# Two cross attentions whose first batch is pulled ahead of batches 1 and 2, with the first loads cut in pieces on two queues

## The reference

```python
x = x + cross_attention_0(layernorm(x), ctx, tau, delta)   # 16 heads of 16 channels, 120 keys
x = x + encoder_block(layernorm(x))                        # self attention, then one of 8 experts per token
x = x + cross_attention_1(layernorm(x), ctx, tau, delta)   # as the first, other weights
x = x + permuted_experts(layernorm(x))                     # groups of 32 tokens, 128 sets
# inside a cross attention:
q = heads(z @ Wq.T + bq); k = heads(c @ Wk.T + bk); v = heads(c @ Wv.T + bv)
scores = (q @ k.T * tau + delta) / 4
out = (softmax(scores) @ v) @ Wo.T + bo
```

## Time and profile before

| | |
|---|---|
| median of 3 runs | 977.71 us (977.0 to 981.29) |
| profiled execution | 980.43 us, span 978.6 us |
| granted TensorE clock, mean | 0.875 |
| busy: PE, DVE, ACT, POOL | 800.0, 501.8, 344.4, 242.9 us |
| first cross attention, first scores at | 60.41 us |
| second cross attention, first scores at | 705.56 us |

### The profile page before, as it was taken

How to read it: one execution, slowest core, us unless ns; L and a number is a source line. 1 busy time by engine, 2 the same in 40 slices (tenths; PEclk the granted TensorE clock), 3 DMA queues, 4 the chain that set the end, 5 groups by cost and what they waited for, 6 DMA issues and landing times.

```text
span 978.6 us, 16232 instructions
## 1 busy us (share of the span) xinstructions
PE 800.0 (82%) x6103; PEld 605.3 (62%) x6103; DVE 501.8 (51%) x1223; ACT 344.4 (35%) x627; POOL 242.9 (25%) x242
## 2 busy tenths in 40 slices
PE   3557989899999999831799999935479888997998
PEld 2335766566665665531699999924356666675865
DVE  3544577876778765422112212125556886444743
ACT  1323544544544544400222222203044456443211
POOL 1512333322234321211211111026234532112000
PEclk9768989999999999965799999978587799657999
DMA  4959465754463663328454566346835550332001
GB/s 150 122 70 190 81 90 72 96 78 79 67 141 63 74 132 126 130 86 129 148 200 163 185 189 171 103 106 77 105 70 78 88 83 25 121 155 88 1 33 54
DMA packets 66896, 103.29 MB, mean 106 GB/s; under 512 B 21614, under 2 KB 56942, under 8 KB 61662
## 3 DMA queue, kind: packets, MB, share of 16 engines
q1 hardware_dynamic: 64403, 97.07, 47.2%
q0 software_dynamic: 2416, 5.19, 2.9%
HBM read 56.61 MB, written 7.28 MB: 65 GB/s over the span
## 4 chain that ended last, share of the span: by engine, by line
PE 64%; DVE 11%; DMA 8%; ACT 5%; issue 4%; POOL 4%; SPq 3%; DVEq 0%; POOLq 0%; ACTq 0%
PE PS L724 9%; PE U L735 8%; PE U L641 7%; PE MB L574 6%; PE MB L662 5%; PE MB L652 4%; PE PS L627 4%; PE MB L604 4%; PE MB L804 3%; PE MB L590 3%; PE MB L814 2%; SPq L1460 2%; DMA y<-yb,pos 2%; DVE nma L1070 2%; DMA QKa<-mTa 2%
## 5 line engine op out<-in xcount | busy, mean ns | idle before, releaser
L1070 DVE TENSOR_REDUCE nma<-MB 128x2 f32<-128x512 f32 (+1 forms) x192 | 124.2, 672 | 40.5 <-PE MB L604 39.7
L900 ACT ACTIVATE Pa<-PS 128x1024 f32<-128x1024 f32 (+1 forms) x96 | 97.4, 1023 | 73.9 <-PE PS L627 73.0
L1305 POOL TENSOR_TENSOR mv<-mv,vec 128x2 f32<-128x2 f32 x48 | 34.7, 723 | 273.9 <-DVE mv L1025 273.8
L604 PE MATMUL MB<-QKa 99*128 99x120 bf16 (+1 forms) x512 | 73.8, 261 | 26.1 <-DVE nma L1070 14.1
L641 PE MATMUL U<-Pa,Vaa 128*32 128x256 f32 (+1 forms) x768 | 91.6, 401 | 0.9 <-ACT Pa L900 0.7
L724 PE MATMUL PS<-mzT,mw 128*128 128x128 f32 x736 | 87.7, 278 | 1.8 <-ACT mzT L921 1.8
L724 PEld LDWEIGHTS PS<-mzT,mw 128*128 128x128 f32 x736 | 85.7, 195 | 2.4 <-issue 2.3
L735 PE MATMUL U<-mw,mdT 128*128 x368 | 83.3, 379 | 2.3 <-DVE mdT L1209 2.3
L604 PEld LDWEIGHTS MB<-QKa 99*128 99x128 bf16 x512 | 40.7, 105 | 59.5 <-DVE nma L1070 21.8
L735 PEld LDWEIGHTS U<-mw,mdT 128*128 128x128 f32 x368 | 68.2, 190 | 11.0 <-issue 2.7
L1217 DVE TENSOR_TENSOR yt<-U,mb 128x256 f32<-128x256 f32 x23 | 9.8, 425 | 123.2 <-PE U L735 123.2
(11 more groups left out here) (194 smaller groups left out, 1442.8 us busy)
## 6 DMA issues: line engine op xcount, KB each, us to landing
mw<-in_mw SPq DMA_DIRECT2D x31, 1024.0 KB, 5.5
QKa<-spa SPq DMA_DIRECT2D x144, 128.0 KB, 5.1
Qb<-spb SPq DMA_DIRECT2D x48, 128.0 KB, 5.3
Oa<-Uba SPq DMA_DIRECT2D x16, 256.0 KB
v<-in_v SPq DMA_DIRECT2D x1, 4096.0 KB, 13.2
v<-in_v SPq DMA_DIRECT2D x4, 1024.0 KB, 11.2
W<-in_W SPq DMA_DIRECT2D x3, 1280.0 KB, 7.0
yb<-yt SPq DMA_DIRECT2D x23, 128.0 KB, 1.7
```

The lines of the kernel that those rows point to most:

```text
L604: i = e.matmul(b[:, keys * j:keys * j + keys], Q[0:99, h0 + j, 128 * qt:128 * qt + 128], K[0:99, h0 + j, 0:keys], start=True, stop=True)
L900: e.activation(p[0:keys, :], ps[0:keys, :], ACT.Exp, scale=0.25).then_inc(sems["exp"], 1)
L1070: e.tensor_reduce(A.nm[qt][:, h0:h0 + heads], b[:, 0:heads * keys].rearrange("p (h s) -> p h s", h=heads), AX.X, ALU.max, negate=True).the ...
L1305: e.tensor_tensor(rs[r][:, 0:2], ve[r][:, 0:2], mhalf[:, 0:2], ALU.pow).then_inc(sems["rs"], 1)
```

## The change

Both cross attentions get another order at their beginning. Of batches 0, 1 and 2 the preparation was interleaved before; now batch 0's norm, keys, queries and maxima stand first, the transposes and query projections of batches 1 and 2 stand between the maxima of batch 0, and the sends of batches 1 and 2 behind the turned maxima of batch 0 (`mt 0`). Keys of batches 2 and 3 (`kp 2`) come behind `mt 0`, and values of the first three batches later. The setting of ones in the value tiles (`va`) becomes a step of its own.

The first loads are cut: of the first weights the columns of k and q come from ScalarE's queue with the vectors, the rest from SP later; the context of batches 0 and 1 comes ahead of the rest; delta comes first. The scratch of delta gets a place of its own, so ScalarE no longer waits for its DMAs.

```diff
-EARLY = (0, 0.213, 0.9)
+EARLY = (0, 0, 0.9)
+EARLY_KEYS = (0, 0, 2.6)
+T_EARLY = ((-2.2, -1.9, -1.0, -0.8, -0.55, -0.3), (-2.1, -1.8, -0.7, -0.5, -0.1, 0.2))
+T_MAX_EARLY = ((-0.85, -0.28), (-1.25, -0.3))
+T_VALUES = -1.2
-T_LOADS = (-3.2, -1.5, -0.5, 0.5, 1.0, 1.6)
+T_LOADS = (-2.25, -1.9, 0.2, 0.6, 1.0, 1.6)
...
-                task(at(T_KEYS[L]), [("kp", n)], [("ks", n)], [("kr", n), ("kd", n)])
-            task(at(T_KEYS[L][1:]), [("vp", n)])
-            task(at(T_CROSS), [("na", n, 0)], [("nb", n, 0)], [("zt", n)], [("qp", n)], [("qs", n)], [("qd", n), ("of", n)])
+                task(at(T_KEYS[L], EARLY_KEYS), [("kp", n)], [("ks", n)], [("kr", n), ("kd", n)])
+            task(at((T_VALUES if m < 3 else T_KEYS[L][1],)), [("vp", n)])
+            task(T_EARLY[m - 1] if m in (1, 2) else at(T_CROSS), [("na", n, 0)], [("nb", n, 0)], [("zt", n)], [("qp", n)], [("qs", n)], [("qd", n), ("of", n)])
...
-        task(at(even(2 * per + 3, *T_MAX[L])), *segments)
+        task(at(even(2 * per + 3, *(T_MAX_EARLY[m - 1] if m in (1, 2) and L != 1 else T_MAX[L]))), *segments)
...
+        ((-2.0,), [[("va", 0)]]),
...
-    out += [("a2",), ("tb", 2), ("wc",)]
-    others = [([(EARLY[b] if b < 3 else b) + t for t in T_BEFORE], [[("bg", b)], [("ba", b)]]) for b in range(NB)]
+    out += [("a2",), ("va", 2), ("tb", 2), ("wc",)]
+    others = [([((0, 1.5, 1.6)[b] if b < 3 else b) + t for t in T_BEFORE], [[("bg", b)], [("ba", b)]]) for b in range(NB)]
...
-            self.dr, self.dr1 = self.tq[0][0:8, 0, 0:CK], self.tq[1][0:8, 0, 0:CK]
-            self.dsp = self.sp3[0][0:8, :, 0, 0:CK]
+
+            d = Area(s.p - 4096, s.p)
+            self.dr, self.dr1 = (d.new(f"dr{tag}_{i}", [128, CK])[64:72, :] for i in range(2))
+            self.dsp = d.new(f"dsp{tag}", [128, 3, CK], BF)[64:72, :, :]
...
-            g.wait_ge(f"d_dsx_{tag(n)}", 48)
...
-                    g.wait_ge("delta", 4 if n < 16 else 8)
...
+        def first_loads(_):
+            for piece, cols in (("k", slice(512, 1024)), ("q", slice(0, 512))):
+                e.dma_start(LW[0].all[:, cols], D["W0"][:, cols]).then_inc(sems[f"d_W0{piece}"], 16)
+            e.dma_start(vec[:, 0:133], D["vec"]).then_inc(sems["d_vec"], 16)
...
         def first_loads(_):
-            e.dma_start(vec[:, 0:133], D["vec"]).then_inc(sems["d_vec"], 16)
+            e.dma_start(AA.dr, D["delta"]).then_inc(sems["d_delta_a"], 16)
             load_x(0)
+            e.dma_start(AA.ctx[:, :, 0:CK2], D["ctx"][:, :, 0:CK2]).then_inc(sems["d_ctx_a0"], 16)
             e.dma_start(idf[:, :], D["idf"]).then_inc(sems["d_idf"], 16)
-            load_weights(0)
...
         def first_attention():
-            attention_loads(AA, "a", 4)
+            delta_rows(AA, "a", 4)
+            stack_rows(AA, "a")
+            e.dma_start(LW[0].all[:, 1024:2560], D["W0"][:, 1024:2560]).then_inc(sems["d_W0"], 16)
             load_x(1)
+            e.dma_start(AA.ctx[:, :, CK2:], D["ctx"][:, :, CK2:]).then_inc(sems["d_ctx_a1"], 16)
+            e.dma_start(AA.sel[:, :, :, :], D["sel"]).then_inc(sems["d_sel_a"], 16)
```

More of the change, by code:

```diff
@@ L74, in pipeline, with at @@
         m, L = n - first, layer(n)
-        e = EARLY[m] if m < 3 else m
-        def at(times):
-            return [(e if times[0] < -2 else m) + t for t in times]
+        def at(times, early=EARLY):
+            return [(early[m] if m < 3 and times[0] < -2 else m) + t for t in times]
         if cross(n):
             if n % 2 == 0:
-                task(at(T_KEYS[L]), [("kp", n)], [("ks", n)], [("kr", n), ("kd", n)])
-            task(at(T_KEYS[L][1:]), [("vp", n)])
-            task(at(T_CROSS), [("na", n, 0)], [("nb", n, 0)], [("zt", n)], [("qp", n)], [("qs", n)], [("qd", n), ("of", n)])
+                task(at(T_KEYS[L], EARLY_KEYS), [("kp", n)], [("ks", n)], [("kr", n), ("kd", n)])
+            task(at((T_VALUES if m < 3 else T_KEYS[L][1],)), [("vp", n)])
+            task(T_EARLY[m - 1] if m in (1, 2) else at(T_CROSS), [("na", n, 0)], [("nb", n, 0)], [("zt", n)], [("qp", n)], [("qs", n)], [("qd", n), ("of", n)])
         else:
@@ L481, in build @@
     names += [f"d_w1{i}" for i in range(3)]
-    names += ["d_o0", "d_o1"] + [f"d_{w}_{t}" for w in ("delta", "ctx", "ones", "dsx", "sel") for t in "ab"]
+    names += ["d_o0", "d_o1"] + [f"d_{w}_{t}" for w in ("delta", "ones", "dsx", "sel") for t in "ab"]
+    names += ["d_W0q", "d_W0k", "d_ctx_a0", "d_ctx_a1", "d_ctx_b"]
     sems = {name: stack.enter_context(nc.semaphore(f"s_{name}")) for name in names}
@@ L512, in landed, with loaded, context @@
         return f"d_{what}{n % 4}", {"q": 96, "m": 16}[what] * (n // 4 + 1)
+    def loaded(what, n):
+        return f"d_W{layer(n)}{what if n < 8 and what in 'qk' else ''}", 16
+    def context(n):
+        return ("d_ctx_b" if n >= 16 else "d_ctx_a0" if n < 2 else "d_ctx_a1"), 16
     def keys_of(n):
@@ L565, in project_in @@
                 rhs, cols = A.ctx[:, :, CK * (n % NB):CK * (n % NB) + CK2], CK2
-                g.wait_ge(f"d_ctx_{tag(n)}", 16)
+                g.wait_ge(*context(n))
             else:
@@ L569, in project_in @@
                 g.wait_ge("z_turned", z_of(n) + 1)
-            g.wait_ge(f"d_W{layer(n)}", 16)
+            g.wait_ge(*loaded(what[0], n))
             g.free(BANKS.free[what, n])
@@ L585, in values_in @@
                 lhs, m = [zT[:, :, 0:128], zT[:, :, 128:256]], 128
-            g.wait_ge(f"d_W{layer(n)}", 16)
+            g.wait_ge(*loaded("v", n))
             g.free(BANKS.free["vp", n])
@@ L984, in vector, with value_ones, delta_parts @@
         g = Gate(e, sems)
[L986 to L992, removed]
+        def value_ones(L):
+            if L == 0:
+                g.wait_ge("d_idf", 16)
+                e.tensor_copy(idb[:, :], idf[:, :]).then_inc(sems["idb"], 1)
+            for v in att(8 * L).Va:
+                e.memset(v[:, :, :, 1:32:2], 1.0).then_inc(sems["va"], 1)
+        def delta_parts(A, t):
             k = 0 if t == "a" else 4
@@ L1004, in second_attention @@
             g.wait_ge("down_mm", NTILE)
-            ones_and_delta(AB, "b")
+            delta_parts(AB, "b")
         def query_bias(L):
@@ L1324, in offset @@
             res = (x if cross(n) else y)[:, two(n % NB), :]
-            g.wait_ge(f"d_W{layer(n)}", 16)
+            g.wait_ge(*loaded("o", n))
             g.wait_ge(*normed(n))
@@ L1414, in attention_loads, with delta_rows @@
                         ).then_inc(sems[f"d_ones_{t}"], 16)
+        def delta_rows(A, t, delta):
             g.wait_ge("delta", delta)
@@ L1430, in second_attention @@
             g.wait_ge("own", 6)
-            attention_loads(AB, "b", 8)
+            e.dma_start(AB.dr, D["delta"]).then_inc(sems["d_delta_b"], 16)
+            e.dma_start(AB.ctx[:, :, :], D["ctx"]).then_inc(sems["d_ctx_b"], 16)
+            stack_rows(AB, "b")
+            delta_rows(AB, "b", 8)
+            e.dma_start(AB.sel[:, :, :, :], D["sel"]).then_inc(sems["d_sel_b"], 16)
         def loads(i):
```

10 lines of the change are left out of this document (4 added, 6 removed).

## The result

The changed kernel takes 992.05 us (median; 986.79 to 996.41), 1.0135 times the kernel before (95% interval 1.0101 to 1.0169). That is slower by 1.35%; the forecast was 976.5 us and its range ended at 985. The profiled execution is the quickest of these (986.79 us, span 984.4), so its trace shows only 6 of the 14.7 us by which the medians differ (977.36 for the kernel before beside these runs).

What follows compares the result with a forecast made beforehand. The prediction took first loads, then DMA sends, to bound the cross attentions' beginnings. First attention 1.3 us early and second 0.1 late summed to -1.2 us: 976.5 us against 977.71, range 966 to 985.

Steps and rivals of the forecast that it cites:

- What bounds the kernel: First cross attention's beginning: loads until 14.73 us, then backed-up DMA sends; batch 0's turned maxima, issued at 50.21, land at 60.41.
- The first loads: Kernel start: fewer bytes ahead, first keys at 7.0 us, first send from 24.01 to 16.3, first maxima gain 7.7.
- the sum: Both cross attentions: -1.3 + 0.1 = -1.2 us, against the 977.71 us median, giving 976.5 us.
- What takes the place of the wait: Before batch 0's first maximum: VectorE waits on x of batch 2, start at 37.2, giving back 5 of 7.7 us.
- rival of a kept start: Batch 0's first maximum starts at 32 us, all that follows 5.2 earlier; total 969.7 us; chance 0.35.
- To the turned maxima: First maximum to SP's issue of batch 0's turned maxima: 13.8 us, issue at 51.0, first scores at 53.5.
- What is late next: First attention, behind batch 0's turned maxima: delayed sends put `mx 2 0` at 73.1, `mx 3 2` at 88.8, 4.0 late.
- "15.7": First attention, us of work from `mx 2 0` to `mx 3 2`, where it was 17.5 before.
- that is got back: Behind `mx 3 2`: 6.7 us to batch 2's first scores, at 95.5, 1.3 us early instead of 4.0 late.
- The second cross attention: Gather at 656.5, first maxima 683.2, issue 697.7, `mx 18 0` 717.7, then 17.0 to `mx 19 2` at 734.7, 0.1 late.
- rival of the low clock: Between batch 0's maxima, both attentions: idle TensorE at half clock, issue 4.6 us later; total 983.7 us; chance 0.20.
- the rival's own condition: Low clock decides if TensorE has not regained the high level by the first of two query projections between maxima.

Runs made afterwards that it cites:

- qd2_behind: Kernel before with only batch 2's query sends moved behind batch 0's turned maxima, in both cross attentions; 970.45 us, ratio 0.9924.
- loads_only: Changed kernel (cut loads, delta's own scratch) with the order of before in both cross attentions, ones set at the very start; 983.11 us, ratio 1.0021.
- x_ahead: Changed kernel with x of batches 2, 3 and 4 loaded ahead of batch 0's sends, first attention alone; 989.92 us, ratio 1.0139.
- warm run: Changed kernel with matmuls added where TensorE waits, their results read by nothing; 994.8 us, ratio 1.018.
- after_again: The changed kernel run once more, unedited; 998.22 us, ratio 1.0155 to the kernel before.
- all_behind: Kernel before, loads and projections in place, with 18 sends and batch 1's maxima behind batch 0's turned maxima; 986.43 us, ratio 1.0039.
- order_only: Kernel before with the new order of steps alone, in both cross attentions; 1000.94 us, ratio 1.0176.

## Why the prediction was wrong

**What bounds the kernel** held: the first scores before did wait for the backed-up queue, and moving six sends alone, qd2_behind, brings 0.76%.

**The first loads:** right inside the new order (6.03 for 7.0, 15.31 for 16.3). That they gain by themselves, as the sum implies, is not so: loads_only has ratio 1.0021.

**What takes the place of the wait:** right. VectorE waits for x of batch 2 until 33.76 and the first maximum starts at 38.25, for 37.2 forecast. The rival of a kept start fell here.

**To the turned maxima:** 52.84 for 51.0, and first scores at 54.99 for 53.5.

**What is late next is the step that failed**, in the sizes of two terms between the issue of batch 0's turned maxima and `mx 3 2`: 37.8 us forecast, 43.0 measured. (1) `mx 2 0` at 73.1 was 76.73: the issue was 1.84 us late, and from the next send's issue (53.57) the sends took 23.2 us where 21.4 were counted. Nor had I queued batch 1's maxima behind VectorE's wait on x of batch 4; in x_ahead, without that wait, `mx 2 0` still waits for the sends until 73.61. (2) The "15.7" from there to `mx 3 2` was 19.1: of the 3.4 us, 2.5 are the low clock behind the 9.1 us wait, by the warm run; the other 0.9 stay open. The term behind it, "that is got back", was right in its size (6.67 us to the first scores of batch 2 for 6.7), but started 7.1 us late. So batch 2's scores came 5.7 us late instead of 1.3 early, and place 1 is 8.6 late. Behind the sizes lies one judgement: I knew that the DMA queue would stand empty from 33 to 52 us with 18 sends to come, and held that this delay would be got back before batch 2's first scores. The runs show in its place that it is not: with 18 sends behind, place 1 comes 43.1 to 44.7 us after batch 0's turned maxima in each of seven profiles, 38.6 in the kernel before, and all that delays their issue is added to it.

**The second cross attention** failed in the same step. Gather and first maxima were right to 1 us (657.45 and 683.0 for 656.5 and 683.2). The issue of the turned maxima was 0.6 us late (698.29 for 697.7). The 20 us from there to `mx 18 0` were 24.5 (700.26 to 724.72), and the 17.0 behind them 19.4. Here TensorE's wait for the last sends (5.41 us) shows in the row itself. How much of the 4.5 us is due to the later batches' gathers, which GpSimd issues in the same stretch, was not tried. Place 2 is 7.6 us late for 0.1: counted from the end of the experts, the issue of batch 16's turned maxima is 0.8 us earlier than before (54.0 for 54.8), and the time from there to place 2 is 8.4 longer (44.3 for 36.0).

**The rival of the low clock** was put at the wrong place. Between the maxima of batch 0 only the values and the first transpose ran low (2.03 and 1.06 us); by the two projections TensorE was back at 2.4 GHz (granted clock 0.50 from 42 to 44 us, 0.94 from 44 to 48), and the rival's own condition failed:

```profile
43.75 2.35 PE L588 MATMUL MB<-zTa,W 128*128 128x256 f32 x8
48.61 1.99 PE L588 MATMUL MB<-zTa,W 128*128 128x256 f32 x8 [1.85 <-ACT zTa L857]
```

The clock is low from 72 to 78 us (0.50), behind the wait of 9.12 us, which the rival did not have. The price there was 2.5 us, where the rival had 3.6 in each attention. The Trainium skill (TensorE: Matmul & The Clock Gate, "Part 1: The HAM clock gate") says that an idle array falls to half the clock; the 0.50 behind this wait agrees with it.

**The sum.** At the two places the change costs 16.2 us for a forecast gain of 1.2; the medians lost 14.7 and, in the second set, 17.6. The profiled execution won part back between the places (its turned maxima of batch 3 were 4.3 us late, at 110.0 for 105.7, after 8.6 for batch 2); after_again, at the lower clock there, was still 8.8 late. That a lead or a delay is carried through as a shift holds for the medians, not for each execution.

## What to carry to other kernels

Where a preparation is bound by DMA sends, count how long the queue will stand empty with sends still to come: 11 us more of it, from all_behind to order_only, made the consumer of the last send 11 us later, and in the changed kernel first scores 5.4 us earlier did not help it. A small urgent transfer wants to pass the few sends that are not needed next (6 or 12 here, 0.8 to 1.0% faster), not all of them (18: 0.4% slower), and work that can wait should not stand ahead of its issue. When an early load brings nothing, look in each engine's program order for the next wait that stands ahead of the work it should feed.

## What the runs showed of the hardware

Two executions of the changed kernel with the same place 1 to 0.02 us parted by 4.5 us up to the next turned maxima (109.98 and 114.53), at a granted clock of 0.74 and 1.00 against 0.50 and 0.50 from 96 to 108 us, with TensorE busy for 11.0 and 12.0 of these 12 us.

VectorE's cast of 16 columns in the split of the maxima, 0.17 us in the median, took 1.20 at 74.08 us in the changed kernel, until 75.28, while GpSimd ran a 512-column addition from 74.00 to 75.25; TensorE's turn at 75.55 waited for it. In the kernel before one took 0.76, until 43.14, beside an addition that ended at 43.11. The pairs of rows, changed kernel and before:

```profile
74.00 1.25 POOL L1345 TENSOR_TENSOR x<-x,W 128x512 f32<-128x512 f32 x1
74.08 1.20 DVE L1097 CAST Mha<-nma 128x16 bf16<-128x16 f32 x1
```

```profile
41.85 1.26 POOL L1327 TENSOR_TENSOR x<-x,W 128x512 f32<-128x512 f32 x1
42.38 0.76 DVE L1079 CAST Mha<-nma 128x16 bf16<-128x16 f32 x1
```

The Trainium skill (SBUF — State Buffer, "SBUF: two separate sides") says that the two engines share a pair of ports: when the VectorE instruction runs in a two-port mode or has two inputs from SBUF, whichever starts first holds the pair for its whole instruction and the other is blocked. These times agree with it. No run here shows the mode of the cast, and none took the addition away.
